# Output projection of a two-layer cross-attention: float32 products replaced by three fp16 products, bias added by GpSimd, one K product moved

## The reference

```python
# layer 0
q = split(x @ Wq.T);  k, v = split(text @ Wk.T), split(text @ Wv.T)
k_ip, v_ip = split(ip @ Wk_ip.T), split(ip @ Wv_ip.T)
out = merge(attend(q, k, v)) + merge(attend(q, k_ip, v_ip))
x = out @ Wo.T + bo + x
# layer 1, from the x of layer 0: as above with its own weights, and
text_probs = softmax((q @ k_text.T) * scale)            # over all channels at once
sem = ((text_probs @ text) @ ip.T) * scale              # one term per query and ip row
ip_probs = softmax(scores + 0.5 * sem) * spatial_mask   # the mask: one factor per query
x = (text_out + ip_out) @ Wout + bout + x
```

## Time and profile before

| | us |
|---|---|
| median of 3 runs | 1771.71 (1771.56 to 1772.64) |
| the profiled execution | 1772.63 |
| its span, first to last instruction | 1770.5 |
| TensorE busy | 1752.4 |
| VectorE busy | 1197.7 |
| ScalarE busy | 777.5 |
| GpSimd busy | 426.0 |

### The profile page before, as it was taken

How to read it: one execution, slowest core, us unless ns; L and a number is a source line. 1 busy time by engine, 2 the same in 40 slices (tenths; PEclk the granted TensorE clock), 3 DMA queues, 4 the chain that set the end, 5 groups by cost and what they waited for, 6 DMA issues and landing times.

```text
span 1770.5 us, 51997 instructions
## 1 busy us (share of the span) xinstructions
PE 1752.4 (99%) x22067; PEld 1422.1 (80%) x22067; DVE 1197.7 (68%) x2905; ACT 777.5 (44%) x1569; POOL 426.0 (24%) x523
## 2 busy tenths in 40 slices
PE   8999999999999999999999999999999999999999
PEld 4778888888888888887577888888888888888885
DVE  6877676767676767555745567767676767676674
ACT  3334545454545455544322343534353445344342
POOL 3034242424333333321100122122121212122111
PEclk9999999999999999999999999999999999999999
DMA  8652535343434343435147142423142323223221
GB/s 320 122 169 97 167 109 159 109 135 111 133 112 133 112 132 116 129 122 182 60 67 190 37 124 75 115 62 105 45 137 52 116 69 113 59 88 102 82 66 47
DMA packets 124015, 198.37 MB, mean 112 GB/s; under 512 B 41752, under 2 KB 110760, under 8 KB 116936
## 3 DMA queue, kind: packets, MB, share of 16 engines
q1 hardware_dynamic: 118600, 168.44, 32.9%
q10 hardware_dynamic: 5184, 26.60, 4.0%
HBM read 133.91 MB, written 60.88 MB: 110 GB/s over the span
## 4 chain that ended last, share of the span: by engine, by line
PE 92%; DVE 3%; ACT 2%; DMA 1%; issue 1%; POOL 0%; SPq 0%; ACTq 0%
PE proj L559 64%; PE proj L519 7%; PE pv L706 6%; PE st L683 5%; PE rows L663 4%; PE rows L559 3%; PE rows L664 2%; ACT arena L1092 1%; DMA arena<-k_dram 1%; DVE wparts L1419 1%; PE rows L751 1%; DMA extra<-x_dram 0%; DMA k_dram<-arena 0%; PE rows L714 0%; ACT arena L1091 0%
## 5 line engine op out<-in xcount | busy, mean ns | idle before, releaser
L559 PE MATMUL proj<-w_hl,cbuf 128*128 128x128 f16 x9600 | 600.9, 219 | 0.0
L559 PE MATMUL proj<-cbuf,w_hl 128*128 128x322 f16 (+1 forms) x3840 | 591.5, 300 | 0.3 <-DVE arena L1609 0.3
L559 PEld LDWEIGHTS proj<-w_hl,cbuf 128*128 128x128 f16 x9600 | 548.6, 98 | 3.3
L559 PEld LDWEIGHTS proj<-cbuf,w_hl 128*128 128x128 f16 x3840 | 367.7, 97 | 163.5 <-DVE arena L1609 0.6
L1331 POOL TENSOR_TENSOR arena<-arena 128x400 f16<-128x400 f32 x240 | 234.0, 975 | 878.2 <-ACT arena L1092 878.2
L1091 ACT ACTIVATE arena<-st,rs 128x400 f16<-128x400 f32 x480 | 287.3, 599 | 267.6 <-DVE st L1735 158.4
L1067 ACT ACTIVATE arena<-proj 128x323 f16<-128x323 f32 (+1 forms) x160 | 70.7, 442 | 494.6 <-PE proj L559 494.6
L1092 ACT ACTIVATE arena<-st,rs 128x400 f32<-128x400 f32 x480 | 285.8, 595 | 0.0
L1654 DVE TENSOR_TENSOR arena<-arena 128x400 f16<-128x400 f32 x240 | 141.6, 590 | 118.1 <-ACT arena L1092 114.7
L706 PEld LDWEIGHTS pv<-arena 128*128 128x128 f16 x3840 | 175.3, 97 | 25.1 <-issue 4.3
L1735 DVE TENSOR_TENSOR st<-st,sem_t 128x400 f32<-128x400 f32 x240 | 135.4, 579 | 87.1 <-PE st L683 85.4
(11 more groups left out here) (169 smaller groups left out, 1635.4 us busy)
## 6 DMA issues: line engine op xcount, KB each, us to landing
arena<-k_dram SPq DMA_DIRECT2D x240, 185.2 KB, 3.6
k_dram<-arena SPq DMA_DIRECT2D x160, 161.2 KB, 1.9
raw<-ctx_dram SPq DMA_DIRECT2D x16, 1290.0 KB, 7.3
c_dram<-cbuf SPq DMA_DIRECT2D x16, 1290.0 KB, 6.2
cbuf<-c_dram SPq DMA_DIRECT2D x14, 1290.0 KB, 6.3
cbuf<-w_dram ACTq DMA_DIRECT2D x24, 640.0 KB, 8.2
arena<-q_dram SPq DMA_DIRECT2D x48, 125.0 KB, 2.6
w_hl<-w_dram ACTq DMA_DIRECT2D x8, 640.0 KB, 11.4
```

The source lines that it names most:

```text
L559: mm = nc.tensor.matmul(out, x[a](k), w[b](k), start=(k == 0 and m == 0), stop=(k == KT - 1 and m == 2))
```

## The change

- **Output products.** TensorE runs each as three fp16 matmuls: weight high x output high, high x low, low x high. The weighted sums go to `o_hl`, an fp16 view of `qo`: ScalarE writes the high part from the transposed row, VectorE the low part (`o_low_part`), and VectorE's instruction now frees the row.
- **A unit per batch row.** The weighted sums are normalised to a unit of their row (`ounit`, from `top`), so that they fit fp16; the mask's maximum is needed for it (`mask_unit`, a new small input `mask_row`). The copy out of PSUM has a factor per batch row and becomes four instructions of 100 columns.
- **The output weight** is loaded raw into `cbuf[:, 0]` in both layers. In layer zero the load moves from step (6, 2) to (6, 4), in layer one it stays at (6, 4). Its scale chain runs in the last batch row: five `wo_part` and `wo_max` in step (7, 0), the turn and `wo_scale` in (7, 1), high and low parts in (7, 1) and (7, 2). The load of layer one's Q weight, to the same place, moves from (7, 2) to (7, 3).
- **The bias** is added to the residual beforehand by GpSimd (`add_bias`): in layer zero in steps 17, 18 and 37, 38, in layer one ahead of the steps.
- **The K product.** `last` is 4 except in the steps that are `late` (layer zero, g = 1, i < 7).

```diff
@@ views @@
-        wo = (raw[:, 0:CT * C].rearrange("p (c k n) -> p c k n", c=CT, k=CT), wq)
+        wo_raw = cbuf[:, 0, 0:2 * CT * C].bitcast(F32).rearrange("p (c n) -> p c n", c=CT)
+        wo_hl = [t.rearrange("p (m c n) -> p m c n", m=2, c=CT) for t in (
+            raw[:, 0:CT * C].bitcast(F16), t_hl[:, :, :, :].rearrange("p m k t -> p (m k t)")[:, 0:2 * CT * C])]
+        o_hl = qo[:, :, :].rearrange("p c t -> p (c t)").bitcast(F16).rearrange("p (c r m s) -> p c r m s", c=CT, r=B, m=2)
@@ SyncE, bulk, layer zero @@
-                    if g == 2 and i == B - 2:
+                    if g == 3 and i == B - 2:
                         split_done(sp, B - 1)
-                        sp.dma_start(wo[0], wo_d[0]).then_inc(wo_in, 16)
-                    if g == 3 and i == B - 2:
                         sp.dma_start(x_raw, x_d[1]).then_inc(x_in[1], 16)
-                    if g == 2 and i == B - 1:
+                    if g == 4 and i == B - 2:
                         sp.wait_ge(c_out[0], 32 * B // 2)
+                        sp.wait_ge(v_full, 2 * (STEPS - G))
+                        sp.dma_start(wo_raw, wo_d[0]).then_inc(wo_in, 16)
+                    if g == 3 and i == B - 1:
+                        sp.wait_ge(o_low, CT)
                         sp.dma_start(wq, wq_d[1]).then_inc(wq_in, 16)
@@ TensorE, out_tile @@
-                    if half == 0:
-                        pe.wait_ge(wo_in, 16 * (l + 1))
-                if half == 0 and c < 2:
-                    pe.wait_ge(v_low, 2 * (l + 1) * STEPS - 1 + c)
-                linear(wo[l], qo[:, :, half * MT:(half + 1) * MT], "out", l, half, c, ks=ks)
+                if half == 0:
+                    pe.wait_ge(o_low, CT * l + c + 1)
+                    if c < 2:
+                        pe.wait_ge(v_low, 2 * (l + 1) * STEPS - 1 + c)
+                bank, full = bank_ready(pe, "out", l, half, c)
+                out = bank[:, 0:MT].rearrange("p (r s) -> p r s", s=S)
+                rs4 = slice(half * B // 2, (half + 1) * B // 2)
+                for k in ks:
+                    for m, (a, b) in enumerate(((0, 0), (0, 1), (1, 0))):
+                        mm = nc.tensor.matmul(out, wo_hl[l][:, a, c, k * P:(k + 1) * P], o_hl[:, k, rs4, b, :],
+                                              start=(k == 0 and m == 0), stop=(k == CT - 1 and m == 2))
+                    if k == CT - 1:
+                        mm.then_inc(full, 1)
@@ TensorE, window @@
+                if g == 1 and i == B - 1:
+                    turn(os, o_chain, 5 * l + 1, "wo", l)
                 v_tile(n, 2)
...
-                last = 3 if l == 0 else 4
+                last = 3 if late else 4
@@ ScalarE @@
-                nc.scalar.activation(qo[:, g, i * S:(i + 1) * S], rows[:, 0, 0:S], ACT.Copy).then_inc(row_free, 1)
+                nc.scalar.activation(o_hl[:, g, i, 0, :], rows[:, 0, 0:S], ACT.Copy).then_inc(o_hi, 1)
+
+            def wo_high(l, c):
+
+                act.wait_ge(o_chain, 5 * l + 5)
...
+                nc.scalar.activation(wo_hl[l][:, 0, c], wo_raw[:, c], ACT.Copy, scale=os[:, 4:5]).then_inc(o_high, 1)
@@ GpSimd @@
+            def add_bias(l, half, c):
+
+                x = xq[1][half]
+                if l == 0:
+                    pool.wait_ge(x_in[half], 16 + 16 * half)
+                nc.gpsimd.tensor_tensor(x[:, c, :], x[:, c, :], bias[:, l, c:c + 1].to_broadcast([P, MT]),
+                                        ALU.add).then_inc(x_biased, 1)
@@ VectorE @@
-                nc.vector.scalar_tensor_tensor(x[:, c, :], bank[:, 0:MT], bias[:, l, c:c + 1], x[:, c, :],
-                                               ALU.add, ALU.add).then_inc(free, 1)
+                dve.wait_ge(x_biased, CT * (2 * l + half + 1))
+                dve.wait_ge(o_units, l + 1)
+                for n in range(B // 2):
+                    r = half * B // 2 + n
+                    last = nc.vector.scalar_tensor_tensor(x[:, c, n * S:(n + 1) * S], bank[:, n * S:(n + 1) * S],
+                                                          oscale[:, r:r + 1], x[:, c, n * S:(n + 1) * S], ALU.mult, ALU.add)
+                last.then_inc(free, 1)
+
+            def o_low_part(u):
+
+                i, g = u // G % B, u % G
+                dve.wait_ge(o_hi, u + 1)
+                nc.vector.tensor_tensor(o_hl[:, g, i, 1, :], rows[:, 0, 0:S], o_hl[:, g, i, 0, :],
+                                        ALU.subtract).then_inc(row_free, 1)
+
+            def wo_part(l, c):
+
+                dve.wait_ge(wo_in, 16 * (l + 1))
+                nc.vector.tensor_reduce(oparts[:, c:c + 1], wo_raw[:, c], AX.X, ALU.max,
+                                        apply_absolute_value=True).then_inc(o_parts, 1)
...
+            def wo_low(l, c):
+
+                dve.wait_ge(o_high, CT * l + c + 1)
+                nc.vector.scalar_tensor_tensor(wo_hl[l][:, 1, c], wo_raw[:, c], os[:, 4:5], wo_hl[l][:, 0, c],
+                                               ALU.mult, ALU.subtract).then_inc(o_low, 1)
@@ VectorE, window @@
+                wo_parts = iter(range(CT) if i == B - 1 and g == 0 else ())
+
                 def context_work(count):
                     for _, c in zip(range(count), parts):
                         context_part(i + 1 + (g == G - 1), c)
+                    for _, c in zip(range(count), wo_parts):
+                        wo_part(l, c)
...
                 if more:
                     v_unit(n, 0)
+                if u % STEPS:
+                    o_low_part(u - 1)
                 add_semantic(u, 4)
```

More of the change, by code:

```diff
@@ L207, in xattn_pair_kernel @@
         y_out = sem("y_out")
+        o_parts, o_chain, o_high, o_low, o_units = (sem(f"wo_{n}") for n in ("parts", "chain", "high", "low", "units"))
+        o_hi, mask_in, mask_steps, tops, x_biased = sem("o_hi"), sem("mask_in"), sem("mask_steps"), sem("tops"), sem("x_biased")
         def need(eng, s, n):
@@ L446, in bulk @@
                         sp.wait_ge(v_full, 2 * (LAYERS * STEPS - G))
-                        sp.dma_start(wo[1], wo_d[1]).then_inc(wo_in, 16)
+                        sp.dma_start(wo_raw, wo_d[1]).then_inc(wo_in, 16)
             for n, (a, b) in enumerate(X_PIECES):
@@ L1122, in window @@
                 splits = iter(SLICES[4 * (g - 1):4 * g] if l == 0 and i < B - 1 and g in (1, 2) else ())
+                chunks = iter(((0, 1, 2, 3), (4,))[g - 1] if i == B - 1 and g in (1, 2) else ())
                 def split():
@@ L1126, in split @@
                         split_context(r + 1, k)
+                        break
+                    for c in chunks:
+                        wo_high(l, c)
                         break
@@ L1350, in window @@
                     after = ()
+                biases = iter(())
+                if l == 0 and i in (3, B - 1):
+                    biases = iter({2: (0, 1, 2), 3: (3, 4)}.get(g, ()))
                 for j in range(NT):
@@ L1355, in window @@
                             chore()
+                            break
+                        for c in biases:
+                            add_bias(0, int(i == B - 1), c)
                             break
@@ L1381, in _ @@
                     clear_tiles(l)
-                    for c in range(CT):
-                        bank_done(pool, "out", 0, 1, c)
+                    for half in range(2):
+                        for c in range(CT):
+                            bank_done(pool, "q", 1, half, c)
+                        for c in range(CT):
+                            add_bias(1, half, c)
                 pool.wait_ge(kt_out[0], 96 * (l + 1))
@@ new lines, in mask_unit @@
+            def mask_unit():
+                dve.wait_ge(mask_in, 16)
+                nc.vector.tensor_reduce(munit[:, 0:1], mask_row[:], AX.X, ALU.max,
+                                        apply_absolute_value=True).then_inc(mask_steps, 1)
+                dve.wait_ge(mask_steps, 1)
+                nc.vector.tensor_scalar(munit[:, 0:1], munit[:, 0:1], TINY, None, ALU.max).then_inc(mask_steps, 1)
+                dve.wait_ge(mask_steps, 2)
+                nc.vector.tensor_scalar(munit[:, 1:2].bitcast(I32), munit[:, 0:1].bitcast(I32), EXP_BITS, None,
+                                        ALU.bitwise_and).then_inc(mask_steps, 1)
+                dve.wait_ge(mask_steps, 3)
+                nc.vector.tensor_scalar(munit[:, 0:1], munit[:, 1:2], 2.0, None, ALU.mult).then_inc(mask_steps, 1)
+                nc.vector.tensor_scalar(mask[:, 0:1], mask[:, 1:2], 0.5, None, ALU.mult).then_inc(mask_steps, 1)
@@ L1756, in low @@
                         context_low(i + 1, c)
+                        break
+                    for c in chunks:
+                        wo_low(l, c)
                         break
@@ L1770, in window @@
                     context_scale(i + 1)
+                if g == 1 and i == B - 1:
+                    wo_scale(l)
                 if l == 0 and g == 2 and i < B - 1:
@@ L1823, in window @@
                     context_max(i + 1)
```

(4 more changed lines are left out.)

56 lines of the change are left out of this document (45 added, 11 removed).

## The result

The changed kernel takes 1786.16 us in the median of 6 runs (1782.01 to 1788.17), the kernel before 1771.72 us (6 runs, 1770.91 to 1772.64). The ratio is 1.0075, 95% interval 1.0064 to 1.0087: slower, 5 us above the forecast of 1781 us and inside its range. The profiled execution took 1787.2 us, its span is 1785.4 us; before, the span was 1770.5 us.

The account below looks back on a forecast made before the run. TensorE was taken as the bound, busy 1752.4 of 1770.5 us. The terms, -18.3 - 5.3 + 9.6 + 11.1 + 3.5 + 8.4 = +9.0 us on the profiled 1772.63, gave about 1781 us in the median, range 1773 to 1788.

Parts of the forecast that it names:

- A: Steps 35 and 75: the pauses come but don't lower TensorE's clock; 1777.5 us, chance 0.20.
- D: Only one pause: layer zero's weight comes early enough, issued before step 36's K spread; about 1769 us, chance 0.10.
- Rival C: Faster: weight there when VectorE asks, or TensorE finds other work, so neither pause comes; 1756.5 us, chance 0.08.
- Rival B: Longer waits: layer zero's transfers one behind the other (+3), subtraction in every layer one step (+4); 1787 us, chance 0.16.
- The pauses: Steps 35 and 75: VectorE waits for the output weight and TensorE behind it; 11.1 and 9.6 us lost.
- The clock: Behind the waits in steps 35 and 75 TensorE runs at half rate; 1.75 us each, 3.5 us lost, bounds 0 and 8.
- The output products: Both layers' 100 products as three fp16 matmuls instead of float32: 16.4 us plus 1.9 for small groups, 18.3 us gained.
- The K product: Moved ahead of the fourth maxima in 31 steps of layer zero: 0.17 us wait saved each, 5.3 us gained.
- The smaller terms: Six small costs, including the output's subtraction, copies, scale chain, bias and end; together 8.4 us lost, bounds 4 and 14.
- that first term: Output's added VectorE subtraction: 7 x 0.25 us in layer one's fifth steps, 7 x 0.2 in layer zero's late steps; elsewhere hidden.
- The third term: Scale, five high and five low parts in the last row's second and third steps, mostly layer one: 2.0 us lost.
- TensorE's idle time: Sign to look for in the changed profile: TensorE idle near 20 us more.

Follow-up runs that it names:

- experiment 3: Changed kernel with the output weight's transfer named one step earlier in the sync queue's list, both layers, VectorE's list unchanged: 1763.72 us, ratio 0.9956.
- experiment 4: Changed kernel with redundant matmuls in the pauses of steps 35 and 75: 1786.18 us, ratio 1.0081; with the remaining waits filled too: 1782.46 us, ratio 1.0063.
- experiment 5: Changed kernel with layer zero's output weight issued ahead of the last context half's store in the sync queue: 1783.61 us, ratio 1.0064.
- experiment 6: Changed kernel with weight transfer one step earlier and last output's low part behind next weight's maxima: 1758.14 us; three more edits 1756.63, another maxima order 1756.68.
- experiment 1: Changed kernel with layer zero's last output low part behind the maxima of layer one's first weight in VectorE's list: 1783.94 us, ratio 1.0063.
- experiment 2: Changed kernel with the output weight's whole scale chain one step later in both layers, transfer issued as before: 1766.69 us, ratio 0.9972.
- experiment 7: Kernel before with only the K product moved ahead of the fourth maxima in layer zero's steps that split no context: 1766.07 us, ratio 0.9967.

## Why the prediction held, and where it was off

- **The forecast** named the mechanism, and experiments 3 to 5 showed it: VectorE asks in steps 35 and 75 for a weight that lands 14.7 and 12.7 us into the step, and TensorE misses what is queued behind. Steps 35 and 75 lost 24.1 us against 24.2 forecast. Rivals A and D are out: the clock falls, and both pauses come. Rival C, told as decided by a landing before 4.3 us into the step, is what experiment 3 built: forecast 1756.5, measured 1763.7 us; with the wait between the layers taken out too (experiment 6), which C's sum did not have, 1758.1.
- **Rival B's number, 1787 us, is nearer to the measured 1786.2 than the forecast's 1781**, but neither of its two mechanisms is in the traces: in layer zero the weight landed 10.3 us after its issue, not behind the store's whole transfer, and plain steps of layer one take 17.29 us (17.30 before). The time came near B's by the wait between the layers, which B did not have. That the forecast's own time is within 5.2 us is in part luck as well, since terms below were off both ways.
- **The pauses, 11.1 + 9.6 = 20.7 us** forecast, 20.0 measured with the clock held. In layer zero the issue at 4.4 us into the step was right and the landing 1.2 us sooner than worked out (10.3 us after the issue, not 11.5): the second of two context loads was a fair but slightly long model.
- **The clock, 3.5 us**: 4.3 us, right in kind, a little small. The stretch at half clock outlasted the waits by more than was worked out: it ended 6.2 us behind the start of the first K product in step 35 and 2.4 us behind it in step 75. At half clock that costs 3.1 and 1.2 us, where 1.75 was put on each.
- **The output products, -18.3 us**: about -17.0. Summed from starts without the waits, the records of all output products took 68.6 us before and take 51.7. The pitch is as forecast, 12.85 us for 75 against 16.95 for 50; the 1.9 us put on small groups came only in part:

```profile
868.31 12.85 PE L572 MATMUL proj<-qo,raw 128*128 128x400 f16 x75
```

- **The K product, -5.3 us**: -5.9 alone; plain steps of layer zero take 17.28 us against 17.47 (forecast 17.30).
- **The smaller terms, 8.4 us.** In the first, the fifth steps of layer one came nearly as forecast (19.35 to 19.65 us, 7 x 0.30 for 7 x 0.25), but the 7 x 0.2 us of the late steps did not: 18.1 us before and after. Step 17 lost 0.66 us at GpSimd's low part (forecast 0.5). The third term, 2.0 us for the scale and the parts, is 0.5 us in step 36 and 0.9 in step 76. The others were not measured one by one.
- **TensorE's idle time** was to grow by near 20 us and grew by 28.0: 18.6 are in steps 35 and 75, 3.3 at the weight's turn between the layers, 2.1 in the fifth steps of layer one, 1.8 behind step 79 and 1.5 at a K spread in step 11.
- **The step that failed** is a sentence in that first term: the subtraction costs something in two kinds of steps, and "Elsewhere VectorE has a gap there, [...] where it hides." Behind step 39 it doesn't hide. It waits 3.1 us for a transpose that stands behind Q products on TensorE, and the next weight's maxima stand behind it. I priced the new instruction by its length, 0.25 us, where its wait counts, and looked at its place within a step only, not at the one call outside the loop. Measured: 5.0 us (experiment 1), about the size of the forecast's whole error of 5.2 us in the median. The other differences are smaller and go both ways: +1.3 us by the output products, +0.8 of clock, -0.7 in the pauses, -1.4 in the late steps, -0.6 by the K product, -0.6 in the third term, and +1.3 us that step 11 of the profiled execution is longer by a wait for a K spread, which comes in some executions only (below).

## What to carry to other kernels

An instruction that needs a transfer and stands in a busy engine's list makes all that is queued behind it wait for the transfer, so the question is not where the data is used but where its first reader stands; compare that time with the issue plus the landing, store ahead included. When an instruction is given a second stage on another engine, walk through every place where it is called: the price is the wait that it brings into that engine's order. And move the issue before the reader: one digit in the queue's list of each layer was worth 22 us here.

## What the runs showed of the chip that was not expected

- **The granted clock falls behind shorter waits than I thought.** Two waits of 1.09 and 1.53 us with 0.39 us of work between them were followed by 3.7 us at about half clock (experiment 4). In the kernel of experiment 5 a single wait for a K spread, in step 10, was followed by the same: a granted clock of 0.50 between 326 and 329 us, and twelve matmuls in 3.33 us, where they take 1.82.

```profile
325.34 0.39 PE L687 MATMUL rows<-arena 96*128 96x512 f16 x1 [1.83 <-DMA arena<-k_dram]
325.56 0.26 PE L688 MATMUL rows<-arena 96*128 96x229 f16 x1
325.66 3.33 PE L583 MATMUL proj<-cbuf,w_hl 128*128 128x323 f16 x12
```

Single waits of 1.33 us (step 9 of experiment 3), 1.45 us (step 11 of the changed kernel) and 1.56 us (between the layers in experiment 2) left the clock full. The Trainium skill, in "TensorE: Matmul & The Clock Gate", section "HAM oscillation — how this bites in real kernels", tells of the fall behind waits on transfers that are longer than these in its example. That work behind such a wait starts at half clock agrees; here a shorter one was enough, and the measurement decides.
- **A pause may make the time uncertain, not only long; this is a sign and not shown.** The half clock lasted 13.6, 10.2 and 3.4 us in the changed kernel, and step 35 took 30.24 us there and 28.73 in experiment 1, with the same code in it. The runs of the kernel before and of those in experiments 6 and 7, whose clock stays full behind the start, lie within 2.3 us each, those of the changed kernel and of experiments 1 and 2 within 6.2 to 6.3. But experiment 3, with a stretch at half clock, lies within 1.5 us, and experiment 5, with both pauses, within 2.6, in 4 runs each.
- **Of two large transfers issued 0.5 us apart the second takes longer**: 1600 KB took 8.5 us with a store of 1290 KB behind it and 10.1 to 10.6 with the store ahead, in the five runs that have it so. In layer one, with no store beside it, it took 6.8 to 9.3 us, so that 8.5 can't be told from its time alone.
- **The K spread is late in some executions**, in one of the steps 8 to 11: in six of the ten profiles with the new output products TensorE waited between some 1.2 and 1.8 us there, in the others not; what the spread meets there was not looked into.
